# A windowed-attention stage on one Trainium2 core: the attended values ahead of the scores, the second half of the turned probabilities ahead of the values' projection

## The chip, the cores and the metric

The kernel runs on one core of one Trainium2 chip. The metric is the device time of the whole program in microseconds (us), the median of several runs. Beside it stands one profiled execution, whose trace gives every instruction's start and duration on each engine: TensorE (PE, with its weight loads shown apart as PEld), VectorE (DVE), ScalarE (ACT), GpSimd (POOL) and SyncE (SP), which issues most DMAs.

## What is computed

Two layers over x of shape (16, 56, 56, 128), all in f32. The change lies in the first one, shifted-window attention with 4 heads of 32, on windows of 7 x 7 = 49 tokens:

```
x = jnp.roll(x, (-3, -3), axis=(1, 2))            # x: group-normalised
q, k, v = jnp.split(x @ w_qkv, 3, axis=-1)        # to windows: (b, 4, 64, 49, 32)
dots = jnp.einsum('bhwid,bhwjd->bhwij', q, k) * scale
dots = dots + bias[None, None, None] + MASK[None, None]
attn = jax.nn.softmax(dots, axis=-1)
out  = jnp.einsum('bhwij,bhwjd->bhwid', attn, v)  # the attended values
out  = out @ w_out + b_out                        # rolled back, and added to x
```

The second layer, on the 3136 tokens of each image, is a causal linear attention (`t + num / den`), and then a recurrence `yt = sigmoid(wx_t + yt @ V.T)` with a batch normalisation ahead of it.

## The kernel before

The program has three stages one behind the other: window attention (about the first 764 us of the profiled execution, and the part that the change touches), linear attention, and the recurrence. The engines' programs are written out by hand, one function for each, and they meet only through semaphores.

**The unit of work** of window attention is one row of 8 windows of one image, 8 x 49 = 392 tokens. There are 16 images x 8 rows = 128 units (`NU`). Every engine runs a loop of steps (`pipeline`), and in step n it works on several units at once, each at another place of its way. For unit n the way is as follows, with the line of each instruction:

- POOL normalises the tokens (L580). PE multiplies them with the keys' weights (L279, in step n-1), the queries' (L270) and the values' (L286, four matmuls, one for each pair of windows). ACT copies keys (L498, two instructions) and queries (L505) out of PSUM. The values are copied half by ACT (L517) and half by DVE (L453), two instructions each, DVE's after ACT's.
- PE makes the scores (L304, 16 matmuls in 64 x 64 corners of the array). DVE adds the bias (L461), which takes them out of PSUM, and finds each row's peak (L469). POOL subtracts it (L587, one step later), ACT takes the exponential (L523), DVE adds up and inverts (L424, L430, two steps later), and POOL weighs (L594).
- Three steps later PE turns the probabilities in two halves of four transposes each (L320). Both halves go into the same PSUM bank (`b_pt`), and ACT copies each to SBUF (L529). PE then makes the attended values out of them (L336, 16 matmuls that use 128 rows and 64 columns of the array), ACT copies these (L538, L539, L540), and one step later PE multiplies with the output weights (L351, 3 matmuls on even units and 4 on odd ones), and DVE adds the input tokens (L440), after which SP stores the unit.

Every f32 matmul is two PE instructions in the trace, each with a weight load of its own (a transpose is one). Each PSUM destination is there once: a unit's values wait in the bank `b_v` until both ACT and DVE have copied the unit before (`at_least(pe, v_out, n)` ahead of L286), the scores' two banks until L461 has read them (`biased`), and the second half of the turned probabilities waits until ACT has copied the first (`p_out` ahead of L320). DVE's order in a step is: aggregate (every eighth step), L424, L430, L440, L391 (statistics of a unit to come), group variance (every eighth step), L461, L469, L453. In one step of eight PE also has the small matmul L263, for the group statistics.

The last 3 of the 128 steps, and 6 more in which the pipeline runs empty, carry steps of the linear attention beside them (`JOIN`).

Of the kernel before, what the change touches and what calls it, by code (L numbers as in the profile page):

```python
# [39 lines left out]
def at_least(eng, sem, value):  # L40

    if not isinstance(value, int) or value > 0:
        eng.wait_ge(sem, value)
# [17 lines left out]
def inside(n, count):  # L61

    return not isinstance(n, int) or 0 <= n < count
# [41 lines left out]
def window_attention(nc, x_cm, x_tok, x1, w_qkv, w_out, b_out, shift_mask_d, position_d, ident_d, group_d, own_d,  # L105
# [3 lines left out]
    if True:  # L109
# [71 lines left out]
        def tiles_in(k):  # L181

            return slice(0, NTILE - 1) if k % 2 == 0 else slice(NTILE - 1, WS)
# [23 lines left out]
        if True:  # L207
# [44 lines left out]
            def _(pe):  # L252
# [19 lines left out]
                def keys(n, k):  # L272
                    if inside(n, NU):
                        if n == 0:
                            pe.wait_ge(first_consts, 64)
                            pe.wait_ge(pool_blank, 1)
                        pe.wait_ge(normed, n + 1)
                        at_least(pe, k_out, n)
                        nc.tensor.matmul(b_k[:, 0:ROWTOK], wqkv[:, C:2 * C], xn[:, k % S, :, 0:WIN], start=True, stop=True).then_inc(k_ready, 1)  # L279

                def values(n, k):
                    if not inside(n, NU):
                        return
                    at_least(pe, v_out, n)
                    for p in range(PAIRS):
                        mm = nc.tensor.matmul(b_v[0:LANES, p * C:(p + 1) * C], xn[:, k % S, 2 * p:2 * p + 2, :].rearrange("p w c -> p (w c)")[:, 0:LANES],  # L286
                                              wqkv[:, 2 * C:3 * C], start=True, stop=True)
                    mm.then_inc(v_ready, 1)
# [19 lines left out]
                def turn_probabilities(n, k, h):  # L308
                    if not inside(n, NU):
                        return  # L310
                    if n == 0:
                        pe.wait_ge(first_consts, 64)
                        pe.wait_ge(pool_blank, 3)
                    if h == 0:
                        pe.wait_ge(weighted, n + 1)
                    at_least(pe, p_out, n * 2 + h)
                    for p in range(2):
                        for hp in range(2):
                            q = p * 2 + hp
                            mm = nc.tensor.transpose(b_pt[:, q * LANES:(q + 1) * LANES],  # L320
                                                     prob[0:LANES, k % S, hp, 2 * h + p].rearrange("p j c -> p (j c)"),
                                                     ident[0:LANES, 0:LANES])
                    mm.then_inc(p_turned, 1)
# [17 lines left out]
                def project(n, k):  # L341
                    if not inside(n, NU):
                        return
                    if n == 0:
                        pe.wait_ge(late_consts, 64)
                    pe.wait_ge(o_out, n + 1)
                    at_least(pe, summed, n)
                    tiles = tiles_in(k)
                    for i, t in enumerate(range(tiles.start, tiles.stop)):
                        ot = oT[:, k // 2 % 2, 2 * t:2 * t + 2, :].rearrange("p a b -> p (a b)")  # L350
                        mm = nc.tensor.matmul(b_y[0:CH, i * C:(i + 1) * C], ot, wout[:, :], start=True, stop=True)  # L351
                    mm.then_inc(projected, 1)

                def step(n, k):
                    queries(n, k)
                    turn_probabilities(n - 3, k - 3, 0)
                    project(n - 4, k - 4)
                    values(n, k)
                    group_moments(n, k)
                    turn_probabilities(n - 3, k - 3, 1)  # L360
                    scores(n, k)
                    attend(n - 3, k - 3, 0)
                    attend(n - 3, k - 3, 1)
                    keys(n + 1, k + 1)
                released = dict(u=(q_out, NU), qk=(k_out, NU), v=(v_out, NU), at=(biased, NU), kv=(p_out, 2 * NU),
                                num=(o_out, NU), gram=(summed, NU))
# [117 lines left out]
            @block.scalar  # L484
            def _(act):
                nc.scalar.dma_start(group[:, :], group_d).then_inc(first_consts, 16)
                nc.scalar.dma_start(wqkv[:, :], w_qkv).then_inc(first_consts, 16)
                nc.scalar.dma_start(own[:, :], own_d).then_inc(first_consts, 16)
                nc.scalar.dma_start(ident[:, :], ident_d).then_inc(first_consts, 16)
                act.wait_ge(first_consts, 64)  # L490

                def keys_out(n, k):
                    if not inside(n, NU):
                        return
                    act.wait_ge(k_ready, n + 1)
                    at_least(act, scored, n - S + 1)
                    for slot in range(2):
                        last = nc.scalar.activation(kb[:, k % S, slot, :], b_k[:, 0:ROWTOK], ACT.Identity, scale=own[:, slot:slot + 1])  # L498
                    last.then_inc(k_out, 1)

                def queries_out(n, k):
                    if inside(n, NU):
                        act.wait_ge(q_ready, n + 1)
                        at_least(act, scored, n - S + 1)
                        nc.scalar.activation(qT[:, k % S, :], b_q[:, 0:ROWTOK], ACT.Copy, scale=float(HD) ** -0.5).then_inc(q_out, 1)  # L505

                def values_out(n, k):
                    if not inside(n, NU):
                        return
                    if n == 0:  # L510
                        act.wait_ge(pool_blank, 2)
                    act.wait_ge(v_ready, n + 1)
                    at_least(act, attended, (n - S + 1) * 2)
                    for par in range(2):
                        rows_ = slice(par * WPAD, par * WPAD + WIN)
                        src = b_v[rows_, :].rearrange("p (w a b c) -> p w a b c", w=PAIRS, a=2, b=2)[:, :, :, par, :]
                        last = nc.scalar.activation(vb[rows_, k % S, :, par, :, par, :], src, ACT.Copy)  # L517
                    last.then_inc(v_half_out, 1)

                def exps(n, k):  # L520
                    if inside(n, NU):
                        act.wait_ge(lowered, n + 1)
                        nc.scalar.activation(softmax_view(prob, k % S), softmax_view(prob, k % S), ACT.Exp).then_inc(raised, 1)  # L523

                def probabilities_out(n, k, h):
                    if inside(n, NU):
                        act.wait_ge(p_turned, n * 2 + h + 1)
                        at_least(act, attended, (n - S) * 2 + h + 1)
                        nc.scalar.activation(pT[:, k % S, h].rearrange("p a b c -> p (a b c)"), b_pt[:, 0:4 * LANES], ACT.Copy).then_inc(p_out, 1)  # L529

                def attended_out(n, k):
                    if not inside(n, NU):
                        return
                    act.wait_ge(attended, n * 2 + 2)
                    at_least(act, projected, n - S + 1 + (k + 1) % 2)
                    src = b_ot[:, 0:ROWTOK].rearrange("p (w r c) -> p w r c", w=NWC, r=WS)
                    dst = oT[:, k // 2 % 2, k % 2 * WS:k % 2 * WS + WS]
                    nc.scalar.activation(dst[:, :, DISP:W - EDGE].rearrange("p r (w c) -> p w r c", c=WS), src[:, 0:NWC - 1], ACT.Copy)  # L538
                    nc.scalar.activation(dst[:, :, W - EDGE:W], src[:, NWC - 1, :, 0:EDGE], ACT.Copy)  # L539
                    nc.scalar.activation(dst[:, :, 0:DISP], src[:, NWC - 1, :, EDGE:WS], ACT.Copy).then_inc(o_out, 1)  # L540

                def step(n, k):
                    attended_out(n - 4, k - 4)
                    keys_out(n, k)
                    probabilities_out(n - 3, k - 3, 0)
                    queries_out(n, k)
                    values_out(n, k)
                    probabilities_out(n - 3, k - 3, 1)
                    exps(n - 1, k - 1)
                pipeline(step, **run, following=linear["scalar"](act), join=JOIN)  # L550

            @block.gpsimd
# [977 lines left out]
```

## Time and profile before

| | |
|---|---|
| median of 3 runs | 1868.79 us (1865.89 to 1869.9) |
| profiled execution | 1865.68 us, its span 1863.6 us |
| PE busy over the span | 1819.5 us (98%) |
| PEld / DVE / ACT / POOL busy | 1611.6 / 1524.8 / 1216.4 / 1014.2 us |
| 400 to 500 us, inside window attention: DVE / ACT / POOL busy | 88.2 / 80.4 / 83.0 us |
| HBM traffic | 183 MB, 98 GB/s over the span |

The busy share of PE counts matmuls whose ends are modelled and which overlap, so 98% says that PE is seldom without a matmul, and not that it couldn't be faster. For a change of order what matters is when a group of instructions starts, and how far from there the next group starts; these distances are read from the timeline. A row with [x <-ENGINE tile line] says that the engine stood idle for x us and what released it.

### The profile page before, as it was taken

What the parts mean: (1) busy time and instruction counts of PE and PEld (TensorE: products, weight loads), DVE (VectorE), ACT (ScalarE), POOL (GpSimd) and SP (SyncE); (2) the same over time, 40 slices, a digit from 0 to 9 for tenths busy, and PEclk for the clock granted to TensorE, in tenths of its full rate; (3) what the DMA queues carried; (4) which work ended last, traced back from release to release, by engine and by line L of the source; (5) the groups of instructions that cost most, each with busy time, mean ns of one, the idle gap of its engine ahead of it and who ended that gap; (6) DMA issues with size and microseconds to landing.
All of it is one profiled execution on the core that took longest, in us unless ns stands there. A gap on an engine that the chain in (4) does not pass through costs nothing.

```text
span 1863.6 us, 57678 instructions
## 1 busy us (share of the span) xinstructions
PE 1819.5 (98%) x19572; PEld 1611.6 (86%) x19572; DVE 1524.8 (82%) x4707; ACT 1216.4 (65%) x3183; POOL 1014.2 (54%) x1177
## 2 busy tenths in 40 slices
PE   5999999999999999899999999999999998999998
PEld 4888888888888888799999999999999997788886
DVE  6888888888888888688888888888888886566665
ACT  4888888888888888566666666666666665333333
POOL 5888888888888888533333333333333434432331
PEclk9999999999999999999999999999999999999999
DMA  4333333333333332122222222222223222556543
GB/s 147 106 106 106 106 106 106 106 106 106 106 106 106 106 85 80 47 72 68 69 69 66 70 69 64 69 69 67 69 69 92 69 64 83 205 175 221 186 165 126
DMA packets 207875, 186.99 MB, mean 100 GB/s; under 512 B 14696, under 2 KB 191712, under 8 KB 207584
## 3 DMA queue, kind: packets, MB, share of 16 engines
q1 hardware_dynamic: 207008, 182.93, 32.7%
q8 instruction: 164, 2.69, 0.6%
q14 instruction: 127, 1.04, 0.2%
q10 hardware_dynamic: 576, 0.33, 0.1%
HBM read 105.93 MB, written 77.27 MB: 98 GB/s over the span
## 4 chain that ended last, share of the span: by engine, by line
PE 96%; DVE 1%; DMA 1%; ACT 0%; issue 0%; POOL 0%; SPq 0%; DVEq 0%; POOLq 0%; ACTq 0%
PE k_psum L781 9%; PE k_psum L336 7%; PE k_psum L286 6%; PE k_psum L279 6%; PE k_psum L304 6%; PE k_psum L351 5%; PE k_psum L320 5%; PE k_psum L1402 5%; PE k_psum L1393 5%; PE k_psum L832 5%; PE k_psum L846 5%; PE k_psum L793 5%; PE k_psum L850 5%; PE k_psum L816 5%; PE k_psum L861 5%; PE k_psum L270 4%
## 5 line engine op out<-in xcount | busy, mean ns | idle before, releaser
L965 POOL TENSOR_SCALAR la_spread<-la_mv 128x4 f32<-128x4 f32 x203 | 46.2, 228 | 481.6 <-DVE la_mv L1069 481.6
L587 POOL TENSOR_TENSOR wa_prob<-wa_prob,wa_peak 128x784 f32<-128x784 f32 x128 | 195.0, 1523 | 119.4 <-DVE wa_peak L469 119.4
L911 ACT ACTIVATE la_ve<-k_psum 128x256 f32<-128x256 f32 x196 | 75.6, 386 | 231.8 <-PE k_psum L793 231.8
L971 POOL TENSOR_TENSOR la_rstd<-la_spread,k_exponent 128x4 f32<-128x4 f32 x203 | 209.9, 1034 | 17.3 <-POOL la_spread L965 0.7
L1461 ACT ACTIVATE sc_y<-k_psum,sc_cols 128x256 f32<-128x256 f32 x208 | 98.6, 474 | 180.8 <-PE k_psum L1402 180.8
L781 PE MATMUL k_psum<-la_uT,la_wt 128*128 128x256 f32 x784 | 201.9, 380 | 0.0
L594 POOL TENSOR_TENSOR wa_prob<-wa_prob,wa_inv 128x784 f32<-128x784 f32 x128 | 195.1, 1525 | 11.3 <-DVE wa_inv L430 11.3
L1025 DVE SCALAR_TENSOR_TENSOR la_fqk<-k_psum,la_raised 128x512 f32<-128x512 f32 x196 | 135.6, 692 | 77.3 <-ACT la_raised L903 77.2
L1189 POOL TENSOR_TENSOR sc_ub<-sc_tb,sc_scan_rstd 128x3584 f32<-128x3584 f32 (+6 forms) x22 | 93.2, 4239 | 175.7 <-PE k_psum L1383 174.0
L461 DVE TENSOR_TENSOR wa_prob<-k_psum,wa_bias 128x784 f32<-128x784 f32 x128 | 124.9, 976 | 74.7 <-PE k_psum L304 74.7
L903 ACT ACTIVATE la_raised<-k_psum,la_minus_one 128x512 f32<-128x512 f32 x196 | 134.8, 688 | 42.9 <-PE k_psum L781 42.7
L517 ACT ACTIVATE wa_vb<-k_psum 49x256 f32<-49x256 f32 x256 | 97.0, 379 | 92.5 <-PE k_psum L286 90.9
L320 PEld LDWEIGHTS k_psum<-k_ident,wa_prob 113*128 113x128 f32 x1024 | 118.5, 142 | 43.5 <-issue 24.6
L498 ACT ACTIVATE wa_kb<-k_psum,wa_own 128x392 f32<-128x392 f32 x256 | 136.5, 584 | 27.7 <-PE k_psum L279 27.7
L846 PE MATMUL k_psum<-la_ve,la_aT 128*128 128x129 f32 x784 | 151.8, 276 | 0.9 <-DVE la_tn L1083 0.9
L832 PE MATMUL k_psum<-la_ve,la_kt 128*128 128x129 f32 (+1 forms) x768 | 150.7, 278 | 1.8 <-ACT la_state L927 1.6
L850 PE MATMUL k_psum<-la_state,la_fqk 128*128 128x129 f32 (+1 forms) x768 | 148.9, 275 | 0.0
L606 POOL TENSOR_TENSOR wa_xb<-wa_xw,wa_bout 112x384 f32<-112x384 f32 (+1 forms) x128 | 146.7, 1146 | 0.0
L336 PE MATMUL k_psum<-wa_pT,wa_vb 128*64 128x49 f32 x4096 | 146.5, 224 | 0.1
L529 ACT ACTIVATE wa_pT<-k_psum 128x452 f32<-128x452 f32 x256 | 140.2, 548 | 8.1 <-PE k_psum L320 5.0
L336 PEld LDWEIGHTS k_psum<-wa_pT,wa_vb 128*64 128x64 f32 x4096 | 130.0, 138 | 17.7 <-ACT wa_pT L529 0.5
L320 PE MATMUL k_psum<-k_ident,wa_prob 113*128 113x113 f32 x1024 | 142.3, 261 | 1.4 <-POOL wa_prob L594 1.4
(137 smaller groups left out, 5294.5 us busy)
## 6 DMA issues: line engine op xcount, KB each, us to landing
wa_xT<-in_x_cm SPq DMA_DIRECT2D x128, 196.0 KB, 3.3
la_xc<-x SPq DMA_DIRECT2D x196, 128.0 KB, 2.1
t<-la_tn SPq DMA_DIRECT2D x196, 128.0 KB, 2.1
sc_tb<-t SPq DMA_DIRECT2D x12, 1792.0 KB, 8.2
out<-sc_ob SPq DMA_DIRECT2D x12, 1792.0 KB, 13.1
wa_xw<-in_x_tok SPq DMA_DIRECT2D x64, 224.0 KB, 2.7
wa_xw<-in_x_tok SPq DMA_DIRECT2D x64, 168.0 KB, 2.3
x<-wa_y SPq DMA_DIRECT2D x64, 168.0 KB, 2.8
```

The source lines that it names most:

```text
L320: mm = nc.tensor.transpose(b_pt[:, q * LANES:(q + 1) * LANES], prob[0:LANES, k % S, hp, 2 * h + p].rearrange("p j c -> p (j c)"), ident[0: ...
L336: mm = nc.tensor.matmul(b_ot[64 * hp:64 * hp + 64, c:c + WIN], vb[:, k % S, h * 2 + w // 2, w % 2, hp].rearrange("p a b -> p (a b)"), pT[: ...
L498: last = nc.scalar.activation(kb[:, k % S, slot, :], b_k[:, 0:ROWTOK], ACT.Identity, scale=own[:, slot:slot + 1])
L529: nc.scalar.activation(pT[:, k % S, h].rearrange("p a b c -> p (a b c)"), b_pt[:, 0:4 * LANES], ACT.Copy).then_inc(p_out, 1)
L587: nc.gpsimd.tensor_tensor(s, s, peak[:, k % S, :].unsqueeze(2).broadcast_to([128, PAIRS * HEADS, WIN]), ALU.subtract).then_inc(lowered, 1)
L594: nc.gpsimd.tensor_tensor(s, s, inv[:, k % S, :].unsqueeze(2).broadcast_to([128, PAIRS * HEADS, WIN]), ALU.mult).then_inc(weighted, 1)
L606: nc.gpsimd.tensor_tensor(xb[:, k, 0:count], xw[:, k, 0:count], bout[:, :].unsqueeze(1).broadcast_to([CH, count, C]), ALU.add).then_inc(x_ ...
L781: mm = nc.tensor.matmul(b_qk[:, j * 2 * P:(j + 1) * 2 * P], wt[:, j * C:(j + 1) * C], uT[:, n % S, :], start=True, stop=True)
L832: nc.tensor.matmul(b_kv[:, 0:E], kt[part, n % S, a, :], ve[part, n % S, a, :], start=fresh, stop=True, skip_group_check=True).then_inc(kv_ ...
L846: mm = nc.tensor.matmul(b_num[:, a * E:(a + 1) * E], aT[:, n % S, a, :], ve[:, n % S, a, :], start=True, stop=begins(c), skip_group_check= ...
L850: mm = nc.tensor.matmul(b_num[0:p, a * E:(a + 1) * E], fqk[:, n % S, 0, a * P:a * P + p], state[:, c % S, :], start=False, stop=True, skip ...
L971: nc.gpsimd.tensor_tensor(rstd[:, n % S, :], spread[:, :], exponent[:, 0:4], ALU.pow).then_inc(rooted, 1)
```

## The change

On PE, the second half of the transposes (L320) goes from behind the values' matmuls to ahead of them, and the scores (L304) go from ahead of the attended values (L336) to behind them. On ACT, the copy of the second half (L529) goes ahead of the copy of the values (L517). Nothing is added or taken away, and DVE, POOL and SP keep their orders.

```diff
@@ PE, step(n, k)
                     queries(n, k)
                     turn_probabilities(n - 3, k - 3, 0)
                     project(n - 4, k - 4)
+                    turn_probabilities(n - 3, k - 3, 1)
                     values(n, k)
                     group_moments(n, k)
-                    turn_probabilities(n - 3, k - 3, 1)
-                    scores(n, k)
                     attend(n - 3, k - 3, 0)
                     attend(n - 3, k - 3, 1)
+                    scores(n, k)
                     keys(n + 1, k + 1)
@@ ACT, step(n, k)
                     keys_out(n, k)
                     probabilities_out(n - 3, k - 3, 0)
                     queries_out(n, k)
+                    probabilities_out(n - 3, k - 3, 1)
                     values_out(n, k)
-                    probabilities_out(n - 3, k - 3, 1)
                     exps(n - 1, k - 1)
```

PE's program in a step with 3 output matmuls, from the output projection (L351) to the last group of the step. A form gives the operand's partitions or columns, x3 means three more such matmuls, and the names behind "waits" are semaphores. Before:

```order
L351 MATMUL k_psum<-wa_wout,wa_oT 112x128 [waits wa_summed,wa_o_out]
L351 MATMUL k_psum<-wa_wout,wa_oT 112x128 x2
L286 MATMUL k_psum<-wa_wqkv,wa_xn 113x128 [waits wa_v_out]
L286 MATMUL k_psum<-wa_wqkv,wa_xn 113x128 x3
L320 MATMUL k_psum<-k_ident,wa_prob 128x113 [waits wa_p_out]
L320 MATMUL k_psum<-k_ident,wa_prob 128x113 x3
L304 MATMUL k_psum<-wa_kb,wa_qT 49x98 [waits wa_biased,wa_q_out,wa_k_out]
L304 MATMUL k_psum<-wa_kb,wa_qT 49x98 x15
L336 MATMUL k_psum<-wa_pT,wa_vb 64x49 [waits wa_p_out,wa_o_out,wa_v_out]
L336 MATMUL k_psum<-wa_pT,wa_vb 64x49 x7
L336 MATMUL k_psum<-wa_pT,wa_vb 64x49 [waits wa_p_out]
L336 MATMUL k_psum<-wa_pT,wa_vb 64x49 x7
```

And in the changed program:

```order
L351 MATMUL k_psum<-wa_wout,wa_oT 112x128 [waits wa_summed,wa_o_out]
L351 MATMUL k_psum<-wa_wout,wa_oT 112x128 x2
L320 MATMUL k_psum<-k_ident,wa_prob 128x113 [waits wa_p_out]
L320 MATMUL k_psum<-k_ident,wa_prob 128x113 x3
L286 MATMUL k_psum<-wa_wqkv,wa_xn 113x128 [waits wa_v_out]
L286 MATMUL k_psum<-wa_wqkv,wa_xn 113x128 x3
L336 MATMUL k_psum<-wa_pT,wa_vb 64x49 [waits wa_p_out,wa_o_out,wa_v_out]
L336 MATMUL k_psum<-wa_pT,wa_vb 64x49 x7
L336 MATMUL k_psum<-wa_pT,wa_vb 64x49 [waits wa_p_out]
L336 MATMUL k_psum<-wa_pT,wa_vb 64x49 x7
L304 MATMUL k_psum<-wa_kb,wa_qT 49x98 [waits wa_biased,wa_q_out,wa_k_out]
L304 MATMUL k_psum<-wa_kb,wa_qT 49x98 x15
```

Ahead of L351 both programs have the keys (L279), the queries (L270) and the first half of the transposes (L320), and behind the last row the next keys. Between the second half of the transposes (L320) and ACT's copy of the first half there is now only the output projection (L351). The scores (L304) stand last, and between them and the next values (L286) lie the keys, the queries, both halves of the transposes and the projection.

DVE's program around the same place, the same in both. L461 waits for the scores, and L453, the second half of the values' copy that `wa_v_out` stands for, comes two instructions behind it:

```order
L461 TENSOR_TENSOR wa_prob<-k_psum,wa_bias 128x16x49 [waits wa_p_turned,wa_scored]
L469 TENSOR_REDUCE wa_peak<-wa_prob 128x16 [waits wa_biased]
L453 COPY wa_vb<-k_psum 49x4x2x32 [waits wa_attended,wa_v_half_out]
L453 COPY wa_vb<-k_psum 49x4x2x32
L424 TENSOR_REDUCE wa_total<-wa_prob 128x16 [waits wa_raised]
```

Nothing moved in these rows; what moved is the group on PE that `wa_scored` counts.

## Rows read from the trace of the kernel before

**Rows 1.** The page, busy time of each engine over the span

```profile
PE 1819.5 (98%) x19572; PEld 1611.6 (86%) x19572; DVE 1524.8 (82%) x4707; ACT 1216.4 (65%) x3183; POOL 1014.2 (54%) x1177
```

**Rows 2.** The page, the chain that ended last, by engine

```profile
PE 96%; DVE 1%; DMA 1%; ACT 0%; issue 0%; POOL 0%; SPq 0%; DVEq 0%; POOLq 0%; ACTq 0%
```

**Rows 3.** Timeline of PE, one step in the middle: start us, us, group

```profile
401.78 0.93 PE L279 MATMUL k_psum<-wa_xn,wa_wqkv 128*128 128x392 f32 x2
...
403.21 0.55 PE L320 MATMUL k_psum<-k_ident,wa_prob 113*128 113x113 f32 x4
...
403.60 0.82 PE L351 MATMUL k_psum<-wa_wout,wa_oT 128*112 128x128 f32 x6
...
404.14 0.94 PEld L286 LDWEIGHTS k_psum<-wa_wqkv,wa_xn 128*113 128x113 f32 x8
...
404.25 1.04 PE L286 MATMUL k_psum<-wa_wqkv,wa_xn 128*113 128x128 f32 x8
...
405.13 0.55 PE L320 MATMUL k_psum<-k_ident,wa_prob 113*128 113x113 f32 x4
...
405.61 0.89 PE L304 MATMUL k_psum<-wa_kb,wa_qT 64*49 64x98 f32 x32
...
406.43 1.14 PE L336 MATMUL k_psum<-wa_pT,wa_vb 128*64 128x49 f32 x32
...
407.50 0.93 PE L279 MATMUL k_psum<-wa_xn,wa_wqkv 128*128 128x392 f32 x2
```

**Rows 4.** Timeline of DVE, the same step

```profile
400.85 0.98 DVE L461 TENSOR_TENSOR wa_prob<-k_psum,wa_bias 128x784 f32<-128x784 f32 x1 [0.70 <-PE k_psum L304]
...
401.86 0.97 DVE L469 TENSOR_REDUCE wa_peak<-wa_prob 128x16 f32<-128x784 f32 x1
...
402.87 0.86 DVE L453 COPY wa_vb<-k_psum 49x256 f32<-49x256 f32 x2
...
405.39 0.56 DVE L391 BATCH_NORM_STATS2 wa_stats<-wa_xT 128x6 f32<-128x392 f32 x1
...
406.57 0.98 DVE L461 TENSOR_TENSOR wa_prob<-k_psum,wa_bias 128x784 f32<-128x784 f32 x1 [0.62 <-PE k_psum L304]
```

**Rows 5.** Timeline of ACT and POOL, the same step

```profile
402.75 1.07 ACT L498 ACTIVATE wa_kb<-k_psum,wa_own 128x392 f32<-128x392 f32 x2 [0.21 <-PE k_psum L279]
...
402.91 1.52 POOL L587 TENSOR_TENSOR wa_prob<-wa_prob,wa_peak 128x784 f32<-128x784 f32 x1 [1.30 <-DVE wa_peak L469]
...
403.80 0.55 ACT L529 ACTIVATE wa_pT<-k_psum 128x452 f32<-128x452 f32 x1
...
404.42 0.68 POOL L580 TENSOR_SCALAR wa_xn<-wa_xT,wa_rstd,wa_shift 128x392 f32<-128x392 f32 x1
```

**Rows 6.** Timeline of the opening, where PE waits for DVE's copy of values

```profile
24.34 1.13 PE L286 MATMUL k_psum<-wa_wqkv,wa_xn 128*113 128x128 f32 x8 [1.59 <-DVE wa_vb L453]
...
25.40 0.89 PE L304 MATMUL k_psum<-wa_kb,wa_qT 64*49 64x98 f32 x32
...
35.10 0.86 DVE L453 COPY wa_vb<-k_psum 49x256 f32<-49x256 f32 x2
...
36.01 0.93 PEld L286 LDWEIGHTS k_psum<-wa_wqkv,wa_xn 128*113 128x113 f32 x8 [1.12 <-DVE wa_vb L453]
...
36.98 0.55 PE L320 MATMUL k_psum<-k_ident,wa_prob 113*128 113x113 f32 x4
...
37.46 0.89 PE L304 MATMUL k_psum<-wa_kb,wa_qT 64*49 64x98 f32 x32
```

**Rows 7.** Timeline of DVE, L461 of unit 3, of two more, and of unit 127

```profile
38.42 0.98 DVE L461 TENSOR_TENSOR wa_prob<-k_psum,wa_bias 128x784 f32<-128x784 f32 x1 [0.87 <-PE k_psum L304]
...
412.50 0.98 DVE L461 TENSOR_TENSOR wa_prob<-k_psum,wa_bias 128x784 f32<-128x784 f32 x1 [0.70 <-PE k_psum L304]
...
459.26 0.98 DVE L461 TENSOR_TENSOR wa_prob<-k_psum,wa_bias 128x784 f32<-128x784 f32 x1 [0.70 <-PE k_psum L304]
...
763.11 0.97 DVE L461 TENSOR_TENSOR wa_prob<-k_psum,wa_bias 128x784 f32<-128x784 f32 x1 [0.52 <-PE k_psum L304]
```

## The prediction

> **What bounds the kernel now.** I read the page first. PE is busy for 98% of the span [rows 1] and makes 96% of the chain that ended last [rows 2]; DVE has 82%. Such shares say whose order matters, not what a step lasts. For that I went to the timeline of one step in the middle of window attention and read it by starts, since a matmul's end is modelled. On PE the groups follow one another without a gap [rows 3]: keys to the first transposes 1.43 us (401.78 to 403.21, the queries between them), transposes 0.39, projection 0.65, values 0.88, second transposes 0.48, scores 0.82, attended values 1.07. That is 5.72 us, and the next keys start at 407.50. PE waits for nobody there. All other engines wait for PE or for one another: DVE 0.62 to 0.70 us in each step for the scores [rows 4], ACT 0.21 for the keys and POOL 1.30 for the peaks [rows 5]. A step with four output matmuls is longer, 5.93 (L461 from 406.57 to 412.50) [rows 4, 7], and in eight steps L263 comes once: 46.76 us from 412.50 to 459.26, 0.16 more than four of each kind. Over the whole stage L461 goes from 38.42 (unit 3) to 763.11 (unit 127), which is 5.844 us for each of 124 steps [rows 7].
>
> So before the change the stage is bound by PE's own stream. The question is whether the same work in the new order still runs without a wait. PE, DVE and ACT are tied by waits in rings that close once a step, and a step can't be shorter than any ring.
>
> **The change part by part.** *PE's own stream.* No instruction is added or removed, so only the borders between groups could change the sum. Going from full-array matmuls to the scores' 64 x 64 ones costs 0.09: the transposes take 0.48 ahead of the scores and 0.39 ahead of the projection [rows 3]. The order before has three borders at which the tile size changes (L320 to L304, L304 to L336, L336 to L279), the new one has three as well (L286 to L336, L336 to L304, L304 to L279). No row shows L286 to L336, L336 to L304 or L304 to L279. From below, a border that costs nothing would give back 0.09. But at all the borders that rows do show, the next group starts 0.07 ahead of the modelled end of the one before, whichever pair it is: 405.13 + 0.55 against 405.61, 405.61 + 0.89 against 406.43, 406.43 + 1.14 against 407.50 [rows 3], 24.34 + 1.13 against 25.40 [rows 6]. From above, a border that waits for the whole modelled end costs 0.07 more. I take the 0.07 ahead, as in every row: the values then take 1.04 - 0.07 = 0.97 to the attended values, these 1.07 to the scores and the scores 0.82 to the keys, and with 0.39 for the second transposes PE's own step is 5.72 and 5.93 as before.
>
> *The ring through DVE.* This is the term that decides. The values of unit n+1 (L286) may not start before DVE has copied unit n's out of the single bank (L453), and DVE copies only behind L461 and L469, which wait for the scores of unit n (L304). Before, the scores stand ahead of the attended values. Now these come between the values and the scores, so 1.07 us come into the ring and only the 0.48 of the transposes leave it. From start to start:
> - scores to L461: 405.61 to 406.57 = 0.96 [rows 3, 4];
> - L461 to L453: 400.85 to 402.87 = 2.02, and the two copies 0.86 [rows 4];
> - end of L453 to PE's weight load: 35.10 + 0.86 = 35.96, L286 loads at 36.01: 0.05 [rows 6];
> - values to the next group of another tile size, when PE has just been released: 24.34 to 25.40 = 1.06 [rows 6]. Without a wait it is 0.97. The other 0.09 is the first weight load, which an unhindered PE makes ahead of time (404.14 for a matmul at 404.25 [rows 3]) and a waiting one doesn't: released at 36.01, the values take 0.97 to the transposes at 36.98, against 0.88;
> - attended values: 406.43 to 407.50 = 1.07 [rows 3], and then the scores start.
>
> The sum is 0.96 + 2.02 + 0.86 + 0.05 + 1.06 + 1.07 = **6.02 us**. Before, the ring was 0.96 + 2.88 + 0.05 + 1.06 + 0.48 = 5.43, under the 5.72 of PE, and so it never showed. L263 lies in the ring, as it lay in PE's stream: 0.16 in eight steps, 0.02 a step. That makes 6.04 against 5.844, which is 0.196 a step, and over 124 steps 24.3 us.
>
> A rule on the 0.09 of the weight load: the Trainium skill (TensorE: Matmul & The Clock Gate, Part 3, "What overlaps and what doesn't") says that weight loads overlap matmuls in flight only if their row groups differ. By that no head start could be lost, the ring would be 5.93, and the next ring below would decide (my second case). The trace speaks against it: the load at 404.14 runs under a projection that uses the same rows.
>
> *The ring through ACT.* The second transposes wait until ACT has copied the first (one bank), and only the projection is left between them. From the keys on: 0.97 to ACT's key copies (401.78 to 402.75), 1.05 to the copy of the probabilities (403.80), 0.55 for it, 0.05 back to PE (taken as DVE's), 0.09 for a load without head start, 0.39 transposes, 0.97 values, 1.07 attended values, 0.82 scores: 5.96 us [rows 3, 5, 6]. It is over PE's 5.72 in the steps with three output matmuls and about level with the others (5.93). Alone it would cost; under 6.02 it is free, and the two don't add up: by PE's time the values could start at 2.62 + 0.09 + 0.39 = 3.10 us after the keys, and DVE's release (0.82 before the keys, plus 0.96 + 2.88 + 0.05) is at 3.07, with the load at 3.16.
>
> *What is late next.* DVE's own work from L453's end to L391's end is 402.87 + 0.86 to 405.95, 2.22 us [rows 4]; with 2.88 it makes 5.10, so it still waits some 0.9 us a step for the scores, and in every eighth step its group statistics have room there. Behind the waiting L286 on PE stand the attended values and scores. ACT's copy of the values moves with them, but ACT has 20% to spare. POOL's L587 follows L469 and starts about 1.1 us later against PE; L580, which the next keys need, ends at 405.10, 2.4 us ahead of them [rows 3, 5], so 1.3 are left. SP's loads wait for POOL and its stores for DVE's L440, both with the same slack as before against the longer step. I cost these at nothing; if POOL's cover were gone, the keys would wait by what it is short. ACT's copy of the attended values (L538) gets its data earlier, but stands behind L523 and ahead of key copies that wait for the keys anyway (0.21): no gain.
>
> *Ends.* In step 3 the scores move from 37.46 - 36.01 = 1.45 us behind the values to 1.06 + 1.07 = 2.13, 0.7 us once. Behind the scores of unit 127 both orders are the same.
>
> The sum is 24.3 + 0.7 = 25.0 us. Against the profiled execution (1865.68, span 1863.6) it gives 1890.7, and against the median of the runs, which lies 3.1 higher, 1868.79 + 25.0 = **1893.8 us**.
>
> **The rivals.** *Second case, the ring through ACT decides.* If PE's weight load loses nothing when it waits for DVE, or DVE comes a little sooner, the step is 5.96 + 0.02 = 5.98, 0.136 more, 17 us over the stage: 1886. For it: only 0.06 us separate the rings. Against it: each piece of 6.02 has a row, and the released load shows its 0.09 [rows 6].
>
> *Third case, dearer borders.* If PE waits at L286 to L336 and at L336 to L304 for the whole modelled end, 0.07 more each, both lie in the ring: 0.14 a step, 17 us on top, 1911. Against it is that four rows of four kinds agree on the 0.07.
>
> *Fourth case, not slower.* The new order puts the values (all 128 rows) next to the attended values (all 128 rows, half the columns), where before came the scores' 64-row corners. If PE passes that border and the next one without any drain, each of them gives back 0.09 and the group of L336 its modelled overhang of 0.07 (1.14 to 1.07): 0.25 a step. The ring is then 5.77, and with 0.02 for L263 5.79 against 5.844: 7 us less, 1862. It decides from 0.20 a step on. Against it: next to L336 the trace shows borders to the 64-row corners and to the full array, and neither is cheaper than the others.
>
> **How the numbers follow.** A measurement of this kernel can tell about 0.2% (3.7 us) from no change. The first case has 0.75, the second 0.12, the third 0.07, the fourth 0.06, of which 0.02 is a change within 0.2% and 0.04 a gain over 0.2%. Slower by over 0.2% is 0.94. The first case's own width is 0.04 us a step from reading starts to 0.01, or 5 us, and 2 us for runs. The range goes from 1881, which takes in the second case, to 1902, which goes half the way to the third; it leaves out the fourth and most of the third.
>
> **What would show it.** In the profile after, PE should wait before L286 for DVE's L453 in nearly all steps, DVE's idle before L461 should grow to some 0.9 us, L461 should follow L461 in 6.02 us in both kinds of step, and L461 of unit 127 should start near 788. If L461's distances are 5.96, the second case holds; if PE waits nowhere, my ring is wrong. A wait of the keys for POOL would be something I costed at nothing.

## The result and the profile after

The changed kernel takes 1891.43 us (median of 4 runs, 1890.88 to 1891.49) against 1867.34 for the kernel before over all runs of this comparison: a ratio of 1.0129, 95% interval 1.0117 to 1.0141, or 24.1 us more (22 to 26). Its profiled execution took 1891.49 with a span of 1889.8. One execution of the kernel before, beside the later experiments, took 2092.59 at a mean granted clock of 0.848 and is in no ratio here.

The page says little of where the 24.1 us went, as before [rows 1, 2]:

```profile
PE 1845.3 (98%) x19572; PEld 1623.4 (86%) x19572; DVE 1525.2 (81%) x4707; ACT 1229.0 (65%) x3183; POOL 1011.3 (54%) x1177
...
PE 97%; DVE 1%; DMA 1%; ACT 0%; issue 0%; SPq 0%; POOL 0%; DVEq 0%; POOLq 0%; ACTq 0%
```

PE is "busy" for 26 us more with the same instructions. Modelled ends and the chain of waits put the loss on PE itself. The list of waits (total us, times, longest) has one entry between 100 and 600 us in which PE waits for another engine, and it names ACT, not DVE:

```profile
PEld k_psum L320 <- ACT wa_pT L529: 7.6, 42, 0.2
```

The starts say more. The timeline of PE in a step of the changed kernel, with the instructions of DVE and ACT that matter to it (start us, duration us), is the counterpart of [rows 3 to 5]:

```profile
405.35 0.90 PE L304 MATMUL k_psum<-wa_kb,wa_qT 64*49 64x98 f32 x32
...
406.18 0.93 PE L279 MATMUL k_psum<-wa_xn,wa_wqkv 128*128 128x392 f32 x2
...
406.31 0.98 DVE L461 TENSOR_TENSOR wa_prob<-k_psum,wa_bias 128x784 f32<-128x784 f32 x1 [0.91 <-PE k_psum L304]
...
407.32 0.97 DVE L469 TENSOR_REDUCE wa_peak<-wa_prob 128x16 f32<-128x784 f32 x1
...
408.32 0.86 DVE L453 COPY wa_vb<-k_psum 49x256 f32<-49x256 f32 x2
...
408.86 0.55 PE L320 MATMUL k_psum<-k_ident,wa_prob 113*128 113x113 f32 x4
...
409.24 0.93 PEld L286 LDWEIGHTS k_psum<-wa_wqkv,wa_xn 128*113 128x113 f32 x8
409.25 1.11 PE L286 MATMUL k_psum<-wa_wqkv,wa_xn 128*113 128x128 f32 x8
409.45 0.55 ACT L529 ACTIVATE wa_pT<-k_psum 128x452 f32<-128x452 f32 x1 [0.33 <-PE k_psum L320]
...
410.30 1.14 PE L336 MATMUL k_psum<-wa_pT,wa_vb 128*64 128x49 f32 x32
...
411.36 0.89 PE L304 MATMUL k_psum<-wa_kb,wa_qT 64*49 64x98 f32 x32
...
412.19 0.93 PE L279 MATMUL k_psum<-wa_xn,wa_wqkv 128*128 128x392 f32 x2
...
412.32 0.98 DVE L461 TENSOR_TENSOR wa_prob<-k_psum,wa_bias 128x784 f32<-128x784 f32 x1 [0.78 <-PE k_psum L304]
```

The way round the ring is: scores to L461 0.96 (405.35 to 406.31), to L453 2.01 (408.32), its end at 409.18, the values' load at 409.24, which is 0.06 later, to the attended values 1.06 (410.30), to the scores 1.06 (411.36). Together 6.01. The values' load starts together with their first matmul, where before it was 0.11 ahead [rows 3]: PE was being held. In this step, one with four output matmuls, the hold costs just that: the matmul at 409.25 comes 0.39 behind the transposes (408.86), as unheld, and then takes 1.05 to the next group and not 0.97. Over the stage, DVE's L461 of unit 3, of a pair around L263, and of unit 127 [rows 7]:

```profile
38.60 0.98 DVE L461 TENSOR_TENSOR wa_prob<-k_psum,wa_bias 128x784 f32<-128x784 f32 x1 [1.69 <-PE k_psum L304]
...
436.38 0.98 DVE L461 TENSOR_TENSOR wa_prob<-k_psum,wa_bias 128x784 f32<-128x784 f32 x1
442.51 0.98 DVE L461 TENSOR_TENSOR wa_prob<-k_psum,wa_bias 128x784 f32<-128x784 f32 x1 [0.21 <-PE k_psum L304]
...
785.94 0.98 DVE L461 TENSOR_TENSOR wa_prob<-k_psum,wa_bias 128x784 f32<-128x784 f32 x1 [0.60 <-PE k_psum L304]
```

From unit 3 to unit 127 it is 747.34 us, 6.027 for each of 124 steps against 5.844: 22.65 us more. L461 of unit 127 starts 22.8 us later. The span grew by 26.2 in these two executions; the other 3.4 are dealt with in the section on the prediction.

### The profile page after: what moved, and what is told of

Its sections match the earlier page's. It is cut to its first block, busy times and chain, and to the rows that moved or that the text cites. A ratio compares the mean times of both kernels' runs of the same rounds, so it can differ in the third digit from the quotient of the medians.

```text
span 1889.8 us, 57678 instructions
## 1 busy us (share of the span) xinstructions
PE 1845.3 (98%) x19572; PEld 1623.4 (86%) x19572; DVE 1525.2 (81%) x4707; ACT 1229.0 (65%) x3183; POOL 1011.3 (54%) x1177
## 3 DMA queue, kind: packets, MB, share of 16 engines
q14 instruction: 129, 1.06, 0.2%
## 4 chain that ended last, share of the span: by engine, by line
PE 97%; DVE 1%; DMA 1%; ACT 0%; issue 0%; SPq 0%; POOL 0%; DVEq 0%; POOLq 0%; ACTq 0%
PE k_psum L781 9%; PE k_psum L336 7%; PE k_psum L286 7%; PE k_psum L320 6%; PE k_psum L279 6%; PE k_psum L304 6%; PE k_psum L351 5%; PE k_psum L1402 5%; PE k_psum L1393 5%; PE k_psum L832 5%; PE k_psum L846 5%; PE k_psum L793 5%; PE k_psum L850 5%; PE k_psum L816 5%; PE k_psum L861 5%; PE k_psum L270 4%
## 5 line engine op out<-in xcount | busy, mean ns | idle before, releaser
L461 DVE TENSOR_TENSOR wa_prob<-k_psum,wa_bias 128x784 f32<-128x784 f32 x128 | 124.9, 976 | 97.3 <-PE k_psum L304 96.6
L781 PE MATMUL k_psum<-la_uT,la_wt 128*128 128x256 f32 x784 | 202.6, 381 | 0.0
L498 ACT ACTIVATE wa_kb<-k_psum,wa_own 128x392 f32<-128x392 f32 x256 | 136.3, 583 | 55.5 <-PE k_psum L279 55.4
L529 ACT ACTIVATE wa_pT<-k_psum 128x452 f32<-128x452 f32 x256 | 140.1, 547 | 45.8 <-PE k_psum L320 45.8
L320 PEld LDWEIGHTS k_psum<-k_ident,wa_prob 113*128 113x128 f32 x1024 | 113.2, 141 | 56.4 <-issue 25.4
L320 PE MATMUL k_psum<-k_ident,wa_prob 113*128 113x113 f32 x1024 | 145.6, 264 | 3.1 <-POOL wa_prob L594 2.4
L336 PE MATMUL k_psum<-wa_pT,wa_vb 128*64 128x49 f32 x4096 | 147.3, 225 | 0.0
L286 PE MATMUL k_psum<-wa_wqkv,wa_xn 128*113 128x128 f32 x1024 | 144.3, 284 | 1.6 <-DVE wa_vb L453 1.6
L336 PEld LDWEIGHTS k_psum<-wa_pT,wa_vb 128*64 128x64 f32 x4096 | 131.1, 139 | 15.5 <-issue 0.6
```

The costliest lines, as they stand in the source:

```text
L336: mm = nc.tensor.matmul(b_ot[64 * hp:64 * hp + 64, c:c + WIN], vb[:, k % S, h * 2 + w // 2, w % 2, hp].rearrange("p a b -> p (a b)"), pT[: ...
L781: mm = nc.tensor.matmul(b_qk[:, j * 2 * P:(j + 1) * 2 * P], wt[:, j * C:(j + 1) * C], uT[:, n % S, :], start=True, stop=True)
```

## The experiments

The theory to be tested is that of the prediction: a step is as long as the longest of PE's own stream (5.72 or 5.93), a ring through DVE and a ring through ACT. Its rivals: only one of the rings matters, or not the waits but the new neighbours on PE cost. The diffs are against the kernel named.

### The turned probabilities alone

```diff
  (against the changed kernel, PE)
                     group_moments(n, k)
+                    scores(n, k)
                     attend(n - 3, k - 3, 0)
                     attend(n - 3, k - 3, 1)
-                    scores(n, k)
```

> One part of the change alone: the second half of the transposes ahead of the values on PE, its copy ahead of the values' copy on ACT; the scores stay ahead of the attended values. Theory (rings): the ring through DVE is then 0.96 + 2.88 + 0.05 + 1.06 = 4.95 us and doesn't bind, but the ring through ACT is there in full (5.96 us), over PE's 5.72 and about PE's 5.93. So L461 follows L461 in 5.95 to 5.97 in both kinds of step, some 0.13 a step more than before, 16 us in all: about 1883. Rival 1 (only the ring through DVE costs): no change, 1867. Rival 2 (the new borders between tile sizes on PE cost, not waits): this kernel has only one new pair, values to scores, which the opening of before has too, so 1867 as well.

Measured: 1879.37, ratio to before 1.0062 (1.0045 to 1.0078), 11.8 us. So this part costs by itself, which neither rival had. The size was expected 4 us too high. The timeline of the first experiment, ACT and PE, then DVE's next scores:

```profile
410.04 0.39 PEld L320 LDWEIGHTS k_psum<-k_ident,wa_prob 113*128 113x128 f32 x4 [0.18 <-ACT wa_pT L529]
410.05 0.61 PE L320 MATMUL k_psum<-k_ident,wa_prob 113*128 113x113 f32 x4
...
410.39 0.93 PEld L286 LDWEIGHTS k_psum<-wa_wqkv,wa_xn 128*113 128x113 f32 x8
410.49 1.04 PE L286 MATMUL k_psum<-wa_wqkv,wa_xn 128*113 128x128 f32 x8
...
412.42 0.98 DVE L461 TENSOR_TENSOR wa_prob<-k_psum,wa_bias 128x784 f32<-128x784 f32 x1 [0.82 <-PE k_psum L304]
...
418.36 0.97 DVE L461 TENSOR_TENSOR wa_prob<-k_psum,wa_bias 128x784 f32<-128x784 f32 x1 [0.71 <-PE k_psum L304]
424.27 0.98 DVE L461 TENSOR_TENSOR wa_prob<-k_psum,wa_bias 128x784 f32<-128x784 f32 x1 [0.82 <-PE k_psum L304]
```

A step with four output matmuls takes 5.94, one with three 5.91. The second transposes, held by ACT, take 0.44 to the values, not 0.39 + 0.09: a held transpose loses 0.05 of head start, and not the 0.09 of the values' matmul. The ring through ACT is 5.92, where 5.96 was expected, and 0.04 x 124 = 5 us is what was expected too much.

### The attended values alone

```diff
  (against the kernel before, PE)
-                    scores(n, k)
                     attend(n - 3, k - 3, 0)
                     attend(n - 3, k - 3, 1)
+                    scores(n, k)
```

> The other part alone: the attended values ahead of the scores; the second transposes stay behind the values, and ACT keeps the order of before. Theory (rings): the attended values' second half now waits for ACT's copy of the second transposes, which stands behind ACT's copy of the values. From the values' weight load it is 1.17 to ACT's values copy, 0.80 to the copy of the probabilities, 0.55, 0.05, then half a group of attended values 0.54 = 3.11, and with DVE's 0.96 + 2.88 + 0.05 the ring is 7.00 us: 1.18 a step more than before, some 145 us, about 2012. Rival 2 (borders): about as the changed kernel, 1891. Rival 3 (only the length of DVE's ring, no wait for ACT): 0.96 + 2.88 + 0.05 + 0.97 + 0.48 + 1.07 = 6.41, 1940.

Measured: 2017.98 (one run), 150 us over before; 2012 was expected. In this experiment the attended values' loads wait for ACT and the values' loads for DVE, in each of the 71 steps between 100 and 600 us. The first two rows are of its waits (total us, times, longest), the others of its timeline:

```profile
PEld k_psum L336 <- ACT wa_pT L529: 38.5, 71, 0.6
PEld k_psum L286 <- DVE wa_vb L453: 37.1, 71, 0.6
```

```profile
413.78 0.98 DVE L461 TENSOR_TENSOR wa_prob<-k_psum,wa_bias 128x784 f32<-128x784 f32 x1 [1.95 <-PE k_psum L304]
420.82 0.98 DVE L461 TENSOR_TENSOR wa_prob<-k_psum,wa_bias 128x784 f32<-128x784 f32 x1 [1.82 <-PE k_psum L304]
```

The step is 7.04 where the ring was worked out as 7.00. The two parts of the change are not additive: this one alone costs 150 us, with the other one beside it 24. The wait for `wa_pT` shows why: with the second transposes left behind the values, the attended values come before their data.

### The ring through DVE opened, and made longer

The values' copy goes ahead of the bias, where it doesn't depend on the scores; and, in another kernel, DVE's statistics go into the ring.

```diff
  (third experiment, against the changed kernel, DVE)
+                    values_out(n, k)
                     add_bias(n, k)
                     find_peak(n, k)
-                    values_out(n, k)
```

```diff
  (fourth experiment, against the changed kernel, DVE)
-                    measure(n + STATS, k + STATS)
                     group_variance(n, k)
                     set_bias(n)
                     add_bias(n, k)
                     find_peak(n, k)
+                    measure(n + STATS, k + STATS)
                     values_out(n, k)
```

> The changed kernel, but DVE copies a unit's values ahead of its bias and peak, not behind them. L453 then no longer waits for the scores, and the ring through DVE is gone; the ring through ACT (5.96) stays. Theory (rings): 5.98 a step instead of the changed kernel's 6.03, 5 to 6 us less than it, about 1885; the values no longer wait for DVE and start right behind the transposes. Rival 1 (only DVE's ring costs): back to 1867. Rival 2 (borders on PE): no change from 1891.

> The changed kernel, but DVE takes the statistics of a unit to come (L391, 0.56 us) between peak and values' copy. Nothing is added, it only moves into the ring through DVE. Theory (rings): 6.01 + 0.55 = 6.56 a step, 0.55 x 124 = 68 us more than the changed kernel, about 1959, with PE waiting for L453 ahead of the values in every step. Rival 2 (borders, DVE's ring has slack as before): L453 had 0.6 us of slack before the change, and with that left nothing is lost, 1891.

Measured: the third 1879.87, ratio 1.0069 (1.0052 to 1.0085), 11.6 us less than the changed kernel and the same as the first experiment's 1879.37. It was expected at 1885, with the 5.96 for ACT's ring that is 0.04 too much. So with DVE's ring gone just ACT's ring is left, in either order of scores and attended values. The rival with DVE's ring alone (1867) and the one of the borders (1891) both fall. The fourth took 1947.46 (one run), 56 us over the changed kernel, where 68 were expected. Its trace lists the wait of the values' load in all 77 steps between 100 and 600 us (PEld L286 for L453, 40.2 us in all), and shows why 68 was too much. Timeline of DVE and PE's load in the fourth experiment:

```profile
411.90 0.97 DVE L469 TENSOR_REDUCE wa_peak<-wa_prob 128x16 f32<-128x784 f32 x1
...
412.79 0.56 DVE L391 BATCH_NORM_STATS2 wa_stats<-wa_xT 128x6 f32<-128x392 f32 x1
...
413.38 0.86 DVE L453 COPY wa_vb<-k_psum 49x256 f32<-49x256 f32 x2
...
414.29 0.93 PEld L286 LDWEIGHTS k_psum<-wa_wqkv,wa_xn 128*113 128x113 f32 x8 [0.51 <-DVE wa_vb L453]
```

From the peak (L469) to L453 it is now 1.48 (411.90 to 413.38), against 1.00 in the changed kernel (407.32 to 408.32): the 0.56 us instruction lengthened the ring by 0.48, as it starts 0.08 ahead of L469's end. The statistics are taken 11 units ahead (`STATS`), so the last 11 of the 124 steps have none: 0.48 x 113 = 54. In the trace, L461 of unit 3 starts at 40.21 and that of unit 127 at 841.84, 801.62 us, which is 54.3 more than the changed kernel's 747.34.

### The ring through ACT opened, and made longer

```diff
  (fifth experiment, against the changed kernel; seventh, the same against the first)
  PE
+                    turn_probabilities(n - 3, k - 3, 0)
                     queries(n, k)
-                    turn_probabilities(n - 3, k - 3, 0)
                     project(n - 4, k - 4)
  ACT
+                    probabilities_out(n - 3, k - 3, 0)
                     keys_out(n, k)
-                    probabilities_out(n - 3, k - 3, 0)
```

The sixth has this and the third's diff. The eighth has the third's diff and this one:

```diff
  (ACT)
                     keys_out(n, k)
+                    queries_out(n, k)
                     probabilities_out(n - 3, k - 3, 0)
-                    queries_out(n, k)
```

> The changed kernel, with the ring through ACT opened and the one through DVE left: PE makes the first half of the transposes ahead of the queries, and ACT copies it ahead of the keys' copy, so that the second half finds its bank free when PE comes to it. Theory (rings): the ring through DVE alone is 6.01 a step, so nothing changes from the changed kernel, 1891, with the loads of the values at L453's end + 0.05 as before. Rival 1 (ACT's ring has a part in the changed kernel's loss): some us less, at most down to PE's own 5.84 a step, 1868. Rival 2 (borders): 1891 too.

> The changed kernel's order of attended values and scores with both rings opened: DVE copies values ahead of bias and peak, and the first half of the transposes and its copy come early. Theory (rings): PE's own stream is what is left, and its step with the new borders (values to attended values, these to scores, scores to keys) is 5.72 and 5.93, as before: 5.85 to 5.88 with the group statistics, which DVE has less room for, so 1867 to 1872. Rival 2 (borders): the new pairs cost 0.18 a step by themselves, so 1889 to 1891 stays.

> The first experiment (second transposes ahead of the values, scores ahead of attended values) with the ring through ACT opened by the first transposes and their copy coming early. Its trace had 5.92 and 5.94 a step, with the second transposes held by ACT in steps with three output matmuls. Theory (rings): neither ring binds, 5.72 and 5.93, back to 1867. Rival (the order of groups on PE costs, and not the wait): 1879 stays.

> The third experiment (DVE's ring opened, ACT's ring bound) with ACT's copy of the queries (L505) moved ahead of its copy of the first transposes, into ACT's ring. A queued copy starts 0.44 after the one ahead of it in the traces, so the second transposes come 0.44 later in all steps. Theory (rings): 5.92 + 0.44 = 6.36 a step, 0.43 x 124 = 54 us over the third experiment's 1880, 1934. Rival (ACT's ring has slack, as the 20% idle time of ACT suggests): 1880.

**Fifth**, 1891.26, ratio 1.0129 (1.0113 to 1.0146): the same as the changed kernel. ACT's ring has no part in its loss, although the list of waits had named ACT alone. Waits of this kernel between 100 and 600 us, and its timeline:

```profile
PEld k_psum L286 <- DVE wa_vb L453: 10.2, 42, 0.2
```

```profile
412.85 0.97 DVE L461 TENSOR_TENSOR wa_prob<-k_psum,wa_bias 128x784 f32<-128x784 f32 x1 [0.79 <-PE k_psum L304]
418.86 0.98 DVE L461 TENSOR_TENSOR wa_prob<-k_psum,wa_bias 128x784 f32<-128x784 f32 x1 [0.92 <-PE k_psum L304]
```

Here the transposes are early in half of the steps, so the wait of the values for L453 becomes long enough to be listed, and the step is still 6.01.

**Seventh**, 1868.6, ratio 1.0007 (0.9998 to 1.0017): no difference from before that this can tell. The first experiment's 11.8 us were ACT's ring, to within that interval. Steps in its timeline are 5.73 and 5.94.

**Sixth**, 1875.6 (1871.68 to 1878.84), ratio 1.0049 (1.0030 to 1.0069). The new neighbours on PE cost next to nothing: in plain steps of its timeline PE runs 5.73 and 5.95, within 0.02 of before and the same as the seventh, which has none of these three pairs:

```profile
410.24 0.98 DVE L461 TENSOR_TENSOR wa_prob<-k_psum,wa_bias 128x784 f32<-128x784 f32 x1 [0.26 <-PE k_psum L304]
416.19 0.98 DVE L461 TENSOR_TENSOR wa_prob<-k_psum,wa_bias 128x784 f32<-128x784 f32 x1 [0.26 <-PE k_psum L304]
421.92 0.98 DVE L461 TENSOR_TENSOR wa_prob<-k_psum,wa_bias 128x784 f32<-128x784 f32 x1 [0.26 <-PE k_psum L304]
```

But it was expected at 1867 to 1872, and its median lies above. From L461 of unit 3 to that of unit 127 it takes 730.7 us, against 725.9 in the seventh and 724.7 before. Part of this stands in its waits: the first transposes, asked for 0.66 us earlier while POOL's weighing comes as late as in the changed kernel, wait for POOL.

```profile
PEld k_psum L320 <- POOL wa_prob L594: 14.3, 32, 1.2
```

That is 32 of 85 steps between 100 and 600 us; in the fifth, with longer steps, it is 2.5 us in 10, and in the seventh, where the scores stand early, it isn't among the longest. The trace is of the shortest of its four runs; why they spread over 7 us is not known.

**Eighth**, 1914.68 (one run), 35 us over the third, where 54 were expected. The longer ring costs, so the rival with slack on ACT falls, but the copy moved in costs less than the 0.44 that I had taken. Timeline of the eighth:

```profile
412.13 1.07 ACT L498 ACTIVATE wa_kb<-k_psum,wa_own 128x392 f32<-128x392 f32 x2 [0.42 <-PE k_psum L279]
...
412.60 0.55 PE L320 MATMUL k_psum<-k_ident,wa_prob 113*128 113x113 f32 x4
...
413.09 0.50 ACT L505 ACTIVATE wa_qT<-k_psum 128x392 f32<-128x392 f32 x1
...
413.47 0.56 ACT L529 ACTIVATE wa_pT<-k_psum 128x452 f32<-128x452 f32 x1
...
414.07 0.40 PEld L320 LDWEIGHTS k_psum<-k_ident,wa_prob 113*128 113x128 f32 x4 [0.48 <-ACT wa_pT L529]
```

From L498 to L529 it is now 1.34 (412.13 to 413.47), against 1.05 [rows 5]: 0.29 a step, and 0.29 x 124 = 36, close to the 35 measured. L505 pushes L529 back by 0.38 (413.09 to 413.47), and 0.09 of that was free. In the kernel before L529 starts 0.59 behind the first transposes (403.21 to 403.80 [rows 3, 5]), and the same 0.59 separates the second ones from their copy in the changed kernel (408.86 to 409.45), where ACT had stood idle. So the copy was waiting for PE's transposes and not for the key copies, behind which ACT could have begun 0.96 after L498 and not 1.05. Here it is 0.87 (412.60 to 413.47), and ACT is what holds it.

No experiment gave a version faster than the kernel before. The best that opening rings can do is to return to PE's own stream, which no reordering here shortened.

## Why the prediction was right

Forecast were 25.0 us more, 1893.8, of a first case in which DVE's ring decides; measured were 24.1, 1891.43. By its terms:

- **PE's own stream stays 5.72 and 5.93.** Right: 5.73 and 5.95 with the new neighbours and both rings opened (sixth). The 0.07 before the modelled end, read from four pairs, held for the new ones: 409.25 + 1.11 against 410.30, and 410.30 + 1.14 against 411.36, 0.06 and 0.08. The third case (dearer borders) and the fourth (free ones) had no part in it.
- **The ring through DVE, 6.02.** 6.01 by each of its pieces, none off by more than 0.01. Of the rule in the Trainium skill (TensorE: Matmul & The Clock Gate, Part 3) that was weighed there: the load of the values starts with its matmul when held (409.24 and 409.25) and 0.10 ahead of it when not, as in the first experiment's 410.39 for a matmul at 410.49, though transposes and values have 113 rows in common. The measurement decides against the rule, and the 0.09 was needed.
- **L263 adds 0.16 in eight steps.** It adds 0.12 (436.38 to 442.51, against 6.01). That is 0.6 of the 1.6 us by which 24.3 was too much; the rest is 0.01 a step.
- **0.7 us once in step 3.** From unit 2's L461 to unit 3's it is 6.13 (32.47 to 38.60) against 5.30 (33.12 to 38.42), 0.8 more. In the total it doesn't show, as the changed kernel's first L461 already started 0.65 earlier in its execution (20.77 against 21.42).
- **The ring through ACT, 5.96, free under DVE's.** Free it was (fifth: no change without it). Its size is 5.92; the term that was off is the head start of a held transpose, 0.05 and not 0.09. Its path was misread too: the first copy of the turned probabilities waits for PE's first transposes, and not for ACT's key copies. Both ways give 2.02 from the keys (0.97 + 1.05, or 1.43 + 0.59), so the sum doesn't suffer; but ACT had 0.09 of slack there, which the eighth experiment found.
- **What is late next.** DVE's wait ahead of L461 rose to 0.91 and 0.78, as said. (Before, it wasn't in each step, as the prediction reads it: the list of waits has it in 65 of some 85 steps between 100 and 600 us.) POOL's cover sufficed; the sixth experiment shows what lies behind it.
- **After unit 127 both orders are the same.** As instructions, yes; as time, not quite. The first matmuls of the linear attention's next piece (L781) start 776.91 before and 800.49 after, 23.58 later, when L461 of unit 127 was 22.83 later, and the next ones 24.25 later (783.43 and 807.68). There the granted clock differs; stretches of 5 us (busy us of PE, PEld, DVE, ACT, POOL, then clock, DMA share and GB/s), before and then after:

```profile
765.00:770.00 5.00, 3.50 (x48) 2.75 (x48) 4.89 (x16) 1.18 (x4) 3.90 (x6) 1.00 0.13 34
770.00:775.00 5.00, 3.38 (x17) 3.07 (x18) 2.79 (x6) 2.57 (x7) 4.92 (x5) 0.68 0.18 49
775.00:780.00 5.00, 4.04 (x50) 3.33 (x49) 2.29 (x7) 1.67 (x4) 0.48 (x1) 0.97 0.18 46
```

```profile
788.00:793.00 5.00, 4.62 (x48) 4.04 (x48) 4.92 (x15) 1.27 (x3) 3.81 (x5) 0.66 0.10 23
793.00:798.00 5.00, 3.26 (x18) 3.02 (x19) 2.65 (x6) 2.40 (x7) 4.92 (x5) 0.71 0.14 41
798.00:803.00 5.00, 4.51 (x42) 3.57 (x40) 1.04 (x3) 1.21 (x3) 0.28 (x1) 0.61 0.18 46
```

Before, the clock was down to half speed for 3.4 us in all (part of two stretches), after for 10.2 (part of three). PE had stood idle for 2.08 us there just ahead, waiting for POOL's weighing ahead of the transposes at 787.95, against 1.09 before; that this idle time brought the clock down is argued and was not tried. The fifth experiment has 0.83 and 0.83 over the two stretches of 10 us there, where the changed kernel has 0.83 and 0.66; with one trace of each, this can be the kernel or the execution. Together this is 1.4 us of the two profiled executions (22.83 to 24.25). Through the linear attention the lag stays 24.2 us. In the first matmuls of the recurrence, whose program is untouched, it grows to 25.2, where the granted clock over 50 us is 0.93 before (1550 to 1600) and 0.90 after (1573 to 1623), and it stays there to the last matmul (1857.95 and 1883.19); the last 1 us arises behind it. Executions of one kernel differ as much: beside the experiments, the kernel before took 1865.4 to 1869.5, the short ones at a mean granted clock of 0.994 to 0.996, the long ones at 0.993 or 0.994. Its profiled execution is a short one, that of the changed kernel is the longest of its four.

- **The sum.** That 25.0 came within 1 us of the 24.1 measured is in part luck. The stage gave 22.8, 2.2 less than forecast, and what came behind unit 127, forecast as nothing, made up for over half of it. Of the 2.4 us between 1893.8 and 1891.43, another 1.5 lie in the median of the kernel before, 1868.79 when the forecast was made and 1867.34 over all runs.

One sign that I had named was badly chosen: that the profile would show PE waiting for L453 in nearly all steps. The list of waits has one such step in the whole trace of the changed kernel, in the opening. The held time is shorter than the modelled end of the transposes ahead (408.86 + 0.55 = 409.41, past the load at 409.24) and so disappears. It was seen in the starts only, and as a wait in the fourth and fifth experiment. And L461, which was to follow L461 in 6.02 in both kinds of step, does so in 6.01.

## What to carry to other kernels

When an engine that never waits is reordered, list the rings, not the waits: for each buffer that is there once, add start-to-start times from its reuse through the other engines and back, and compare with the step. The one wait that the list of the changed kernel named, for ACT, could be removed without any gain; the one that cost the time was not in the list. Moving one group behind another is paid in each ring that the group enters, here 1.07 us less 0.48 in a ring with 0.3 to 0.5 us of slack, though no instruction was added and all other engines idled for a tenth or more of their time. Take such distances from starts, and price an instruction put into a ring by how far it moves the start of the next one, less the slack there, and not by its duration.

## What was not expected of the hardware

- Some instructions that don't depend on the one ahead of them start before that one's end: L391 0.89 us behind the start of L469 (0.97 long) in the fourth experiment; on ACT, in the eighth, L505 starts 0.96 behind the start of the key copies (1.07 long), and L529 0.38 behind L505 (0.50 long). Not all do: L453, which doesn't depend on L469 either, starts 1.00 behind it (407.32 to 408.32). What decides it is not known. Put into a ring, 0.56 us on DVE cost 0.48, and 0.49 us on ACT cost 0.29.
- The head start that a held weight load loses depends on the matmul: 0.09 for the values (two PE instructions for each matmul), 0.05 for a transpose (one).
- With three changes of tile size in each order, PE's step is the same to 0.02 us (5.72 and 5.93 before, 5.73 and 5.95 in the sixth experiment), though other groups meet.
